# Gathers of a tile and scatters of a half body issued one at a time, in an embedding-bag kernel

## What is computed

```python
B, F, V, L, E = (512, 32, 12500, 20, 64)
flat = tables.reshape(F * V, E)
emb = flat[ids + jnp.arange(F)[None, :, None] * V]
mask = (jnp.arange(L) < lengths[..., None]).astype(emb.dtype)
out = jnp.einsum('bfle,bfl->bfe', emb, mask).reshape(B, F * E)
return jnp.nan_to_num(out)
```

## Time and profile before

| | |
|---|---|
| median of three runs | 1190.97 us |
| span of the profiled execution | 1287.7 us |
| TensorE busy | 1118.5 us |
| GpSimd busy | 547.5 us |
| gathers, scatters of results | 413, 40 |
| mean granted TensorE clock | 0.957 |

### The profile page before, as it was taken

One profiled execution on the slowest core, in us unless ns is written; L12 is line 12 of the kernel. 1 busy time (PEld: TensorE's weight loads), 2 busy tenths in 40 slices (PEclk: granted clock), 3 DMA queues, 4 the chain that ended last, 5 costly groups with the idle time before them and its releaser, 6 DMA issues.

```text
span 1287.7 us, 31751 instructions
## 1 busy us (share of the span) xinstructions
PE 1118.5 (87%) x10873; PEld 969.4 (75%) x10873; DVE 992.5 (77%) x2692; ACT 827.6 (64%) x1233; POOL 547.5 (43%) x519
## 2 busy tenths in 40 slices
PE   3379999896988878989979888979789999999996
PEld 1168888785876767778868767868678888888886
DVE  9657788884886867869868867969678898787881
ACT  4257787673756656757747566757557777787780
POOL 4865665556555455555565544555540101000000
PEclk9989999897999988999989989989989999999998
DMA  5324234241433333242414333242413213123120
GB/s 184 116 68 115 60 83 144 74 136 45 135 107 95 117 86 97 81 132 82 143 46 136 106 95 118 82 130 69 134 25 100 58 55 104 47 62 100 35 73 5
DMA packets 63916, 118.38 MB, mean 92 GB/s; under 512 B 30120, under 2 KB 31742, under 8 KB 63840
## 3 DMA queue, kind: packets, MB, share of 16 engines
q1 hardware_dynamic: 46608, 102.19, 25.5%
q0 software_dynamic: 16032, 15.00, 5.9%
q10 hardware_dynamic: 1200, 0.50, 0.2%
HBM read 87.19 MB, written 4.62 MB: 71 GB/s over the span
## 4 chain that ended last, share of the span: by engine, by line
PE 73%; DVE 10%; another core or an unknown queue 7%; ACT 7%; issue 3%; DVEq 0%; POOL 0%; POOLq 0%
PE sums L525 48%; PE pairs L515 19%; PE rest L543 6%; DVE onehot_j L742 3%; ACT counts L470 3%; ACT table L482 2%; DVE gathered L800 1%; DVE onehot_p L740 1%; ACT rest L478 1%; DVE table L751 1%; ACT table L486 0%; DVE table L759 0%; DVEq L796 0%; DVE is_nan L768 0%
## 5 line engine op out<-in xcount | busy, mean ns | idle before, releaser
L525 PE MATMUL sums<-table,counts 128*128 128x192 bf16 x8624 | 909.0, 251 | 0.8 <-issue 0.8
L470 ACT ACTIVATE counts<-pairs 128x588 int16<-128x588 f32 (+1 forms) x968 | 617.0, 650 | 368.9 <-PE pairs L515 262.7
L525 PEld LDWEIGHTS sums<-table,counts 128*128 128x128 fp8e3 x8624 | 776.3, 98 | 55.0 <-issue 0.4
L427 POOL DMA_INDIRECT rows<-tables,row_now x413 | 453.3, 1098 | 376.7 <-issue 206.1
L742 DVE TENSOR_SCALAR onehot_j<-ramp,j_of,worth 128x296 bf16<-128x296 f16 x1848 | 536.3, 353 | 0.0
L515 PE MATMUL pairs<-onehot_j,onehot_p 128*128 128x294 bf16 x1892 | 410.4, 297 | 112.8 <-ACT counts L470 67.3
L740 DVE TENSOR_TENSOR onehot_p<-ramp,p_of 128x768 bf16<-128x768 f16 x308 | 169.9, 552 | 253.7 <-PE pairs L515 172.9
L515 PEld LDWEIGHTS pairs<-onehot_j,onehot_p 128*128 128x128 bf16 x1892 | 178.2, 98 | 187.3 <-issue 107.8
L543 PE MATMUL rest<-table,minus_eye 128*128 128x448 bf16 x352 | 102.5, 373 | 38.2 <-ACT table L482 17.1
L486 ACT ACTIVATE table<-rest 128x896 f32<-128x896 f32 x88 | 80.8, 918 | 35.3 <-remote 23.6
L437 POOL DMA_INDIRECT out_gathered<-gathered,place_now x40 | 42.4, 1061 | 132.3 <-DVE gathered L771 121.0
(11 more groups left out here) (68 smaller groups left out, 79.8 us busy)
## 6 DMA issues: line engine op xcount, KB each, us to landing
table<-tables SPq DMA_DIRECT2D x154, 448.0 KB
rows<-zeros SPq DMA_DIRECT2D x40, 640.0 KB
rows<-tables,row_now POOLq DMA_INDIRECT x413
out_counted<-pooled SPq DMA_DIRECT2D x132, 21.0 KB
rows<-lookup_ids SPq DMA_DIRECT2D x1, 903.0 KB, 8.5
rows<-lookup_lengths SPq DMA_DIRECT2D x1, 903.0 KB, 10.2
out_counted<-pooled SPq DMA_DIRECT2D x44, 1.0 KB
sorted_records<-records,rank POOLq DMA_INDIRECT x40
```

The lines of the kernel that those rows point to most:

```text
L427: nc.gpsimd.indirect_dma_start(out=rows[:, k, l * E:(l + 1) * E], out_offset=None, in_=table_rows, in_offset=bass.IndirectOffsetOnAxis(ap= ...
L470: nc.scalar.activation(dst, src, ACT.Copy).then_inc(counts_saved, 1)
L525: last = nc.tensor.matmul(sums[h][:, k * PARTS * E:(k + 1) * PARTS * E], counts[h][:, j, :, k], parts[:, :, j, :, 1], start=(j == 0 and k ...
```

## The change

In `gather`, every gather of a tile but the first waits for the landing of the one before it, where before only the third and later ones waited, and for the one before the last. In `put`, the second, third and fourth scatter each wait for the landing of the scatter before. The first gather of a tile and the first scatter of a put wait as before. Buffers, counts, order and data are the same.

```diff
                         x = turn(l)
-                        if l > 1:
-                            pool.wait_ge(rows_in[k][x], landed[x] + 16 * sum(turn(i) == x for i in range(l)))
+                        if l:
+                            ahead = turn(l - 1)
+                            pool.wait_ge(rows_in[k][ahead],
+                                         landed[ahead] + 16 * sum(turn(i) == ahead for i in range(l)))
                             pool.sem_inc(fill_begun, 1)
...
-                for k in range(x * SLOTS, (x + 1) * SLOTS):
+                for i in range(SLOTS):
+                    k = x * SLOTS + i
+                    if i:
+                        pool.wait_ge(gathered_stored[x], b * (16 * SLOTS) + 16 * i)
+                        pool.sem_inc(fill_begun, 1)
                     nc.gpsimd.indirect_dma_start(
                         out=out_gathered, out_offset=bass.IndirectOffsetOnAxis(ap=place_now[:, k:k + 1], axis=0),
                         in_=gathered[:, k * E:(k + 1) * E], in_offset=None).then_inc(gathered_stored[x], 16)
```

## The result

The changed kernel takes 1842.16 us (median of four runs, 1840.33 to 1845.28), against 1188.93 us for the kernel before in the same comparison: 1.549 times as long, 95% interval 1.544 to 1.554.

What follows compares the result with a forecast made beforehand. GpSimd's chain of gathers becomes the bound, in place of TensorE: 84.3 + 51 + 1380 + 68 + 3.4 = 1586.5 us, plus 213 makes 1800 on the trace; 1735 us forecast in the metric, range 1590 to 1890 us.

Steps and rivals of the forecast that it cites:

- The sum on the trace: GpSimd's gathers and puts land the last tile at 1586.5 us; with 213 us behind it, the end is 1800 us.
- 373 links: Waits between gathers of one tile on GpSimd: each a whole turnaround of 3.7 us (3.20 to 4.02), 1380 us.
- 8 puts, with the steps on both sides: Puts ahead of the last gather: 8.5 us each from scatters 2.4 us apart, 68 us; steps between tiles 1.3 us.
- From the trace to the metric: Profiled execution 96.7 us over the median: unprofiled time close to 1800 or scaled to 1665; the middle, 1735 us, taken.
- The margin of 116 us: In the kernel before, last gather issued at 958.2 us, its tile added by VectorE at 1074.7 us.
- where it starts: Tile 4 lands at 307 us, its add due at 264.7; from there VectorE waits in adds of long tiles.
- The traffic term: Gather turnaround: at most 0.7 us over a quiet 3.3 now; if from other transfers, some 0.4 us remain after.
- A lone gather that turns round faster: Rival: with one gather in flight a link falls under 2.15 us, giving 1125 us; 2 in 100.
- The rule of the Trainium skill: Rival: a gather's DMA takes 2.08 us; with 0.3 us of restart a link is 2.38 us, 1208 us; 2 in 100.
- The second reading: The skill's 2.08 us follow on the 1.0 us of descriptors, so a gather's turnaround is 3.4 us.
- Half clock: Rival: TensorE falls to half clock in waits and becomes the bound again, some 2050 us in the metric; 5 in 100.
- That the new waits would be met already: Rival: the new thresholds in gathers and scatters are already met, nothing waits, 1191 us; 2 in 100.

Runs made afterwards that it cites:

- the first profile: The kernel before, unchanged, in the profile on which the prediction rests: span 1287.7 us, 97 us over its median.
- one buffer of eight: The kernel before, with gathers one at a time only in buffer 0 and scatters as before: 1318.19 us, 1.105 of before.
- the thin loads: The changed kernel, with only the first 64 columns of the table chunks loaded from feature 1 on: 1786.94 us.
- the two experiments that moved TensorE's work: The changed kernel with all 40 adds three features later, 1709.79 us; the changed kernel with half of the products left out, 1817.24 us.
- the later adds: The changed kernel with all 40 adds three features later (FIRST_ADD = 5, 8): 1709.79 us.
- the profile of 1181.7 us: The kernel before, profiled a second time with no edit: span 1181.7 us, 1183.76 us in the metric.
- its variants from the comparison at 1278 us: The kernel before with each put two tiles earlier, 1267.48 us; the kernel before with all 40 adds one feature later, 1271.34 us.
- Two kernels bound by GpSimd's chain: Gathers one at a time in four buffers of eight, against the kernel before: 1505.62 us; the changed kernel with adds three features later: 1709.79 us.

## Why the prediction was right, point by point

**The mechanism** held: GpSimd's chain of gathers sets the last add, and TensorE's tail follows. The last add waited for the last landing, the tail was 211.7 us for the 213 of the sum, and neither more nor less of TensorE's work ahead of the add moved it forward.

**The sum on the trace** gave 1800 us against 1843.5. Its terms:

| term | predicted | measured |
|---|---|---|
| first gather | 84.3 | 86.8 |
| 373 links | 1380 (3.7 each) | 1340 (3.59 each) |
| 8 puts, with the steps on both sides | 78 | 104 |
| 31 other steps between tiles | 40 | 98 |
| landing of the last gather | 3.4 | 2.5 |
| tail | 213 | 212 |

The measured puts are the distances from a tile's last gather to the next one's first across a put, 12.7 to 13.8 us each. The link was 3% too dear. The scatter was too cheap: 3.0 us and not 2.4, which is half of the 26 us. The row taken for it was of another kind, where the waiting instruction was a plain load; whether that is the reason is not shown. The other half is the step from a put's last scatter to the next gather, 2.5 to 2.9 us and not 1.30. The steps between tiles were mis-sized worst, by 58 us: I took 1.30 us, the step within a pair, without reading a row at a tile's edge. In the changed kernel they are 3.2 us on average ((1542.5 from first to last gather - 1340 - 104)/31). There GpSimd's program waits for the buffer and reads the tile's depth and counts; which of these takes the time is not shown. The change did not make these steps: in the profile on which the prediction rests the same 31 already sum to 90 us. The landing was too dear because I took 0.3 us of restart, the idle time between two gathers with no wait, where 0.8 us pass. The errors of 40 and 87 us partly cancel.

**From the trace to the metric** is the step that failed most: 65 us off a sum that was already 44 us short. The text named the case that came true (the excess of the first profile in TensorE's middle part, so the time "close to 1800") and then took the mean of the two cases. The rows could have decided it. The chain's "another core or an unknown queue" pieces stand, from 295 us on, nearly all ahead of ScalarE's copies, while beside the three longest GpSimd's gathers l and l + 2 stood 3.3 to 3.4 us apart (one pair 4.5), nearly as in quiet places. A loss that sits in one engine's waits doesn't scale another engine's chain. The 1842 us lie 107 us above the forecast, in the upper part of a range that was wide enough for both cases; the width, not the choice between them, kept the number inside.

**The margin of 116 us** was that of the disturbed execution. It changes the forecast little, since the chain ends where it ends, but "where it starts" and any small version of the change would have been wrong: one buffer of eight would have come out at 1197 us and took 1318. The second reason, the add that waits for a put behind two tiles of gathers, was written out in the description of the kernel and not used in the argument. The prediction had VectorE wait in the adds of long tiles; of its 702 us of waiting ahead of the adds, 440 were for puts.

**The traffic term.** I took 0.4 us above a quiet link of 3.3. It was 0.34 above one of 3.25, and the thin loads show that at least 0.16 of it is the bytes of the table's chunks.

**The rivals.** A lone gather that turns round faster: the closest link is 3.15 us, so no. The rule of the Trainium skill ("DMA: Bandwidth & Descriptors", section "Anatomy of one DMA — SWDGE (gpsimd) path") gives 2.08 us for such a DMA. The profile after has 2.1 us at least and 2.5 us in the median from the start of the instruction to the landing, with the 1.0 us of descriptors inside. So neither reading holds as it was written: the 2.08 us are not a turnaround less 0.3 us of restart, and they do not follow on the descriptors. They come close to the shortest landing, and 0.8 us up to the next start come on top. The second reading's 3.4 us is near the measured 3.3 by luck, since it counts the descriptors twice and the restart too short. Half clock: it came (a mean of 0.79 up to the last add, where it had been 0.95), and cost nothing there, by the two experiments that moved TensorE's work. That the new waits would be met already: 373 waits of 2.5 us say no.

**The signs** named in the forecast were there: TensorE 61% busy, clock 0.79, the last add one landing behind the last gather. The mean distance was 3.59 instead of 3.7, the gathers ended at 1629 instead of 1580 us, the scatters stood 3.0 us apart instead of 2.4, and the first starts of tiles were not 1.3 us behind the tile before.

## What to carry to other kernels

Depth in flight is worth its length only on a chain that binds, and then it is worth all of it: count the dependent steps, read the turnaround from two rows of the trace (start of one to start of the one that waited), and multiply. Look for the margin of a side engine in an undisturbed execution, and at the wait that ties it tightest, which can be a buffer release queued behind later work, and not the last transfer. Here work off the chain was slower, later and at half clock at no cost; the work that stands behind the last join is the piece to move ahead of it, as the later adds did for 132 us.

## What the runs showed of the hardware that was not expected

The turnaround of an indirect gather of 128 rows of 256 bytes is the same with one in flight (3.16 to 3.3 us in quiet places) as with two. The turnaround of a scatter of the same size to the device's main memory was 2.9 to 3.0 us. In both, 0.8 us of it pass between the landing and the start of the instruction that waited for it, and 1.0 us is the writing of the descriptors.

The unchanged kernel took 1187 to 1195 us in four comparisons and 1278 us in one (all 19 runs, 1269 to 1288), and its first profile was of the second kind, with 7% of the chain in waits that the profile puts down to nothing it knows (5% in the two profiles of its variants from the comparison at 1278 us). That comparison ran on another chip than the experiments at 1187 to 1195 us; for the first profile no chip is on record, so whether the chip matters is not shown. Two kernels bound by GpSimd's chain, run beside the 1278 us, came close to sums made from the other comparisons (1505.62 us for 1503, 1709.79 for 1700). What causes those waits is open. The longest in the first profile began close to the bursts of four scatters, but the burst is also there in the profile of 1181.7 us, without them.
